# Second products ahead of the transpose in the expert stage of a graph-attention and mixture-of-experts kernel

## What is computed

```python
x = x + _L0_gnn_ref(_layernorm(x), adj, W, b_W, a_vec, b_a)          # graph attention
x = x + _L0_ffn_ref(_layernorm(x)[None], gate_w, gate_b, w1, w2, w3)[0]

# _L0_ffn_ref: 16 experts, hidden width 256, the two best experts of each token
logits = x @ gate_w + gate_b
top_probs, top_idx = top_k(softmax(logits), 2)       # normalized to a sum of 1
h1, h2 = x @ w1[e], x @ w2[e]                        # 128 -> 256, each expert
hidden = silu(h1) * h2
expert_out = hidden @ w3[e]                          # 256 -> 128
out = sum over the token's two experts of weight * expert_out
```

## Time and profile before

| | |
|---|---|
| median of the three runs | 1666.96 us (1665.37 to 1672.87) |
| the profiled execution | 1668.2 us, span 1666.4 us |
| mean granted TensorE clock | 0.985 |
| TensorE busy | 1474.4 us, 88% |
| VectorE busy | 1383.7 us, 83% |
| ScalarE busy | 822.7 us, 49% |
| GpSimd busy | 523.5 us, 31% |
| DMA | 226 GB/s over the span |

### The profile page before, as it was taken

How to read it: one execution, slowest core, us unless ns; L and a number is a source line. 1 busy time by engine, 2 the same in 40 slices (tenths; PEclk the granted TensorE clock), 3 DMA queues, 4 the chain that set the end, 5 groups by cost and what they waited for, 6 DMA issues and landing times.

```text
span 1666.4 us, 25615 instructions
## 1 busy us (share of the span) xinstructions
PE 1474.4 (88%) x8691; PEld 888.1 (53%) x8692; DVE 1383.7 (83%) x1782; ACT 822.7 (49%) x1372; POOL 523.5 (31%) x708
## 2 busy tenths in 40 slices
PE   3808999999999999999999999999999997888780
PEld 2805654554455455445544554554454467888780
DVE  5897999999999999999999998999986764333344
ACT  2704445556556555655565565556566653223230
POOL 2500000002430351326024312602353335555450
PEclk9999999999999999999999999999999999999995
DMA  9884777786787677768867774675521657777647
GB/s 341 333 323 168 258 255 249 246 256 229 240 260 253 221 257 247 249 222 271 260 220 246 253 247 153 209 248 172 193 83 39 160 157 192 228 219 234 203 154 310
DMA packets 145575, 377.32 MB, mean 226 GB/s; under 512 B 19513, under 2 KB 50937, under 8 KB 142649
## 3 DMA queue, kind: packets, MB, share of 16 engines
q1 hardware_dynamic: 125559, 342.35, 62.2%
q0 software_dynamic: 16704, 27.17, 5.7%
q10 hardware_dynamic: 3202, 6.38, 1.0%
HBM read 347.32 MB, written 32.70 MB: 228 GB/s over the span
## 4 chain that ended last, share of the span: by engine, by line
PE 56%; DVE 20%; issue 11%; POOL 5%; DMA 4%; ACT 3%; another core or an unknown queue 1%; ACTq 0%; SPq 0%; DVEq 0%; POOLq 0%
PE pair L1221 33%; DVE ring L1509 10%; PE pair L1206 9%; PE pair L1323 8%; DVE probs L1543 7%; PE pair L1332 2%; DMA X<-in_x 2%; DMA ring<-res_d 1%; POOL X L708 1%; PE pair L1233 1%; POOL ln L783 1%; POOL numT L795 1%; ACT probs L992 1%; ACT probs L1111 1%
## 5 line engine op out<-in xcount | busy, mean ns | idle before, releaser
L1221 PE MATMUL pair<-probs,X 128*128 128x512 f32 x2048 | 1005.1, 608 | 0.0
L992 ACT ACTIVATE probs<-probs,ebias 128x1024 f32<-128x1024 f32 (+1 forms) x576 | 605.5, 1052 | 530.0 <-DVE probs L1543 517.4
L1543 DVE SCALAR_TENSOR_TENSOR probs<-s1row,ns,pair 128x1024 f32<-128x1024 f32 (+1 forms) x576 | 651.6, 1157 | 50.7 <-PE pair L1206 46.3
L1509 DVE CUSTOM_DVE_ANT_0 ring<-urow,stage 128x2048 int8<-128x2048 f16 x235 | 537.2, 2288 | 4.5 <-DMA stage<-in_adj 4.4
L1206 PEld LDWEIGHTS pair<-diag,ring 128*128 128x128 fp8e5 x4096 | 266.1, 99 | 402.3 <-issue 205.7
L1221 PEld LDWEIGHTS pair<-probs,X 128*128 128x128 f32 x2048 | 344.8, 191 | 216.1 <-issue 216.1
L1206 PE MATMUL pair<-diag,ring 128*128 128x128 bf16 x4096 | 325.4, 220 | 74.4 <-ACT diag L1002 45.8
L846 POOL DMA_INDIRECT xd_d<-xres,sloti x120 | 184.5, 1537 | 39.5 <-issue 31.7
L1323 PE MATMUL pair<-probs,ring 128*128 128x128 f32 x1152 | 158.8, 282 | 39.0 <-ACT probs L1105 21.6
L1937 DVE TENSOR_TENSOR probs<-probs,pair 128x256 f32<-128x256 f32 x144 | 60.3, 419 | 145.7 <-ACT probs L1111 103.6
L921 POOL DMA_INDIRECT res_d<-ring x144 | 139.6, 969 | 127.6 <-DVE ring L1945 95.0
(11 more groups left out here) (272 smaller groups left out, 689.5 us busy)
## 6 DMA issues: line engine op xcount, KB each, us to landing
stage<-in_adj SPq DMA_DIRECT2D x470, 512.0 KB
ring<-w_d SPq DMA_DIRECT2D x144, 256.0 KB
ring<-in_adj SPq DMA_DIRECT2D x21, 1024.0 KB
ring<-xd_d SPq DMA_DIRECT2D x144, 65.0 KB
ring<-res_d SPq DMA_DIRECT2D x16, 512.0 KB, 9.9
w_d<-in_L_ffn_w SPq DMA_DIRECT2D x32, 128.0 KB, 4.4
out<-ring ACTq DMA_DIRECT2D x8, 512.0 KB, 6.8
ring<-xmid_d SPq DMA_DIRECT2D x1, 3840.0 KB
```

Source lines behind the costliest of these rows:

```text
L992: act.activation(probs[:, n % PR, 0:wide], probs[:, n % PR, 0:wide], ACT.Exp, bias=ebias[:, j:j + 1], scale=RISE).then_inc(probs_ready, 1)
L1221: m = pe.matmul(acc[q][:, lo:hi], X[:, j, :], probs[:, n % PR, lo:hi], start=(j == 0), stop=(j == NT - 1))
L1509: dve.tensor_tensor_reduce(m, urow[:, c * CH:(c + 1) * CH], edges, CODE, NO_EDGE, ALU.subtract, ALU.max, part[:, k, c:c + 1]).then_inc(pie ...
L1543: dve.scalar_tensor_tensor(out=probs[:, n % PR, 0:wide], in0=s1row[:, q, 0:wide], scalar=ns2[:, j:j + 1], in1=Tp[n % 2][:, 0:wide], op0=AL ...
```

## The change

In all three places the second products of tile i - 2 are issued before the transpose of tile i + 2. Nothing else is changed; the functions called are the same.

```diff
@@ the first 48 tiles
                 if i >= 1:
                     e[i - 1] = expert_of(i - 1)
-                t_x(i + 2, (i + 2) % XS, (i + 2) // XS + 1)
                 if i >= 2:
                     m_y(i - 2, (i - 2) % XS, e[i - 2], i - 2 < 2)
+                t_x(i + 2, (i + 2) % XS, (i + 2) // XS + 1)
@@ the loop of 16 tiles
                     e[u - 1] = expert_of(XS * g + (u - 1))
+                    m_y(i - 2, (u - 2) % XS, e[u - 2], False)
                     t_x(i + 2, (u + 2) % XS, g + 1 if u + 2 < XS else g + 2)
-                    m_y(i - 2, (u - 2) % XS, e[u - 2], False)
@@ the last 16 tiles
                 if i - 1 < ST:
                     e[i - 1] = expert_of(i - 1)
+                m_y(i - 2, (i - 2) % XS, e[i - 2], False)
                 if i + 2 < ST:
                     t_x(i + 2, (i + 2) % XS, (i + 2) // XS + 1)
-                m_y(i - 2, (i - 2) % XS, e[i - 2], False)
```

## The result

The change makes the kernel slightly slower. Its median is 1674.32 us (1670.07 to 1675.89, 16 runs) against 1668.61 us (1663.69 to 1673.21, 16 runs) of the kernel before, timed beside it. The ratio of the runs is 1.0029, with a 95% interval of 1.0016 to 1.0042. That is 4.8 us; the medians differ by 5.7. That lies inside the 0.5% that the prediction called "no change that can be told", but sixteen runs of each tell it from zero.

A forecast was written before the change was run, and what follows sets the result against it. The prediction took TensorE's work and standing still to bound the experts' tiles. Its terms, 0 + 0 + 0 + 2.5 - 0.5 = +2 us on the profiled 1668.2, gave 1670.2, or 1669 us as a median; range 1655 to 1684.

The forecast's parts named there:

- The forecast case: Whole kernel: no change that can be told, within 0.5% (8.3 us), including the change doing nothing; chance 0.60.
- The waits of the second products: TensorE, experts' tiles: second products' waits, now ahead of the transpose, cost nothing to 1 us; taken as 0.
- The later transpose while signals are prompt: Experts' tiles: transpose starts 0.44 us later, but its copy has 1.0 us of cover before its user; cost 0.
- The later transpose when signals are held: Where signals come one by one, the transpose's copy comes 0.8 us later; 0 to 8 us, taken as 2.5.
- ScalarE's idle time before L1105: ScalarE's wait before its copy of the transpose should rise from 4.7 to some 7 to 10 us.
- The earlier second products: Second products start 0.11 us earlier, so VectorE's result copies wait less; gain 0 to 1 us, taken as 0.5.
- The beat stays, nothing moves outside the stretch: Experts' tiles keep their 5.7 us beat of three tiles; attention part and last 42 us stay as they are.
- The test at 36 to 45 us of idle time before L1323: TensorE's idle time before the first products should stay there; under 30, or over 48 with L1105 as releaser, refutes the prediction.
- The slower rival: Transpose's signal comes last and ends the stall: 0.8 us per beat, measurable from 11 of 48; 1680 us, chance 0.22.
- The rival of the broken beat: Experts' tiles: new order breaks the three-tile beat more often, removing a third of TensorE's idle time; 1654 us, chance 0.18.
- What holds the signals: TensorE's signals come late when it works without a gap, 2.0 us in one beat; GpSimd's indirect DMA is a suspect.

The follow-up runs named there:

- waits_only: Kernel before with its order kept; only the second products' two waits put in front of the transpose: 1674.88 us, 0.9989 of the kernel before.
- actstore_a: Order of the change, but results stored by plain DMAs from ScalarE's queue in tile order, without scattering: 1616.29 us, 0.9644 of the kernel before.
- actstore_b: Order of before, but results stored by plain DMAs from ScalarE's queue in tile order, without scattering: 1616.77 us, 0.9645 of the kernel before.
- copy_waits_y: Kernel before, TensorE unchanged; ScalarE's copy of a transpose also waits for the second products' signal: 1680.62 us, 1.0027 of the kernel before.
- x_first: Kernel before with the transpose of tile i + 2 moved ahead of the first products of tile i: 1679.60 us, 1.0019 of the kernel before.
- pace1: Kernel before with one small GpSimd operation behind each indirect store, stores 1.49 us apart: 1660.28 us, 0.9960 of the kernel before.
- deep: Order of before, pipeline one tile longer with more buffers, ScalarE taking the SiLU ahead of the copy: 1665.65 us, 0.9943 of the kernel before.
- pace2: Kernel before with two small GpSimd operations behind each indirect store: 1696.85 us, 1.0186 of the kernel before.

## Why the prediction was right or wrong

- *The sign and the size.* Forecast +2 us, measured +4.8 us: the sign is right, and the forecast is less than half of what came. The forecast case, no change above 0.5%, is what came, and 1674.32 lies in the range of 1655 to 1684. The median of before was also 1.65 us higher in this timing (1668.61).
- *The waits of the second products, 0.* Right: 1.7 us before L1332, and `waits_only` shows no cost in its times.
- *The later transpose while signals are prompt, 0.* Right: the beat at 1506.29, and `actstore_a` against `actstore_b`.
- *The later transpose when signals are held, 2.5 us.* This is the step that was mis-sized. The mechanism is the one described, the signal of the second products overtaking that of the transpose; `copy_waits_y` reproduces the cost with it alone (and `x_first` gave no gain from the opposite). But I counted the places by what L1105 waited in the old order, eight to ten. That row says how often the copy was late when its signal came before the other, and not how often it would be when it comes behind. After the change it waited for L1316 in 41 places, 19.1 us. I also halved the term for places where something else holds the first products. Of 22 us more waiting in these profiles about a quarter, 4.8 us, reaches the end of the kernel. The upper bound, 8 us, held. But it was 10 places of 0.8 us each, and the late copies were four times as many; that most of them cost nothing was not foreseen, so the bound held by luck.
- *ScalarE's idle time before L1105 rises to 7 to 10 us.* Wrong by a factor of three, 26.6 us, for the same reason.
- *The earlier second products, -0.5 us.* No run isolates a gain. VectorE's wait before L1945 fell from 13.0 to 8.0 us as foreseen, and nobody waited for it.
- *The beat stays, nothing moves outside the stretch.* Right: 5.65 us, and the same windows.
- *The test at 36 to 45 us of idle time before L1323.* The 47.2 us missed it, and it was no good test: one profile shows one execution, and the profile of `waits_only`, whose copy is prompt and whose median is no higher, has 48.1.
- *The slower rival.* It was the same mechanism with a larger count, and it is what acts. At its price of 0.8 us, 4.8 us are six beats of 48, below the eleven from which it would have decided; most of the late copies still have cover.
- *The rival of the broken beat.* Nothing of it came by this order; rather the reverse, since the two stretches without a stall in the profile of before have no counterpart after. (The prediction counts one such stretch; another of 19.5 us begins at 1432.7.) The beat can be broken, as by `pace1`, and without the indirect stores it is not there.
- *What holds the signals.* The prediction says that they are late when TensorE works without a gap, and that they come when it has run dry. `actstore_b` has no gap and prompt signals, and `deep` lets most of them out while TensorE works: so neither holds as a rule, and it was the coincidence of one beat. Its suspect, the indirect DMA, is confirmed as far as that the lateness goes with it.
- *The page of the Trainium skill (PSUM — Partial Sum Buffer, Engine vs sequencer instructions).* It says that an increment attached to a matmul fires when this matmul completes. In `actstore_b`, where no indirect DMA runs beside it, the trace agrees to 0.03 us at 1461.74; where these run, ScalarE sees the signal 2.0 us late. The semaphore's own record is late as well, at 1507.51, so it isn't ScalarE that is slow. In a kernel of the first kind the forecast by the rule, no effect of the order, was also measured.

## What to carry to other kernels

The place of an instruction in a queue is also the place of its signal. Before work is reordered "for nothing", compare the start of each consumer with the end of its producer. Where signals come late, whatever is moved behind needs cover for that delay as well, and the wait that it has now doesn't tell what it will have. One profile can't place an effect that is smaller than the spread of a kernel's executions. And where a busy engine's consumers start late though they are idle, look at what runs beside it (here a stream of indirect DMAs on GpSimd) before turning the order round: that was worth up to 60 us (in kernels that leave the scattering out, so it is a bound and no version to take), the order 5. Of the kernels that compute everything, a deeper pipeline (0.9943) or a small gap between the stores (0.9960) beats both the kernel before and the one after.

## What the runs showed of the hardware

- Beside GpSimd's indirect DMAs, which in a row start 1.27 us apart, TensorE's signals reached ScalarE up to 2.0 us late; without them, 0.03. Of TensorE's recorded signals 75% were over 0.1 us late in the kernel before and none in `actstore_b`; ScalarE's and VectorE's came within 0.013 us in every run. The path on which they are held was not found: the stores differ from the plain ones in the engine that issues them and in how they are made, and both were changed at once.
- With the stores 1.98 us apart (`pace2`) all recorded signals of TensorE came within 0.06 us; with 1.49 us (`pace1`) 72% were still over 0.1 us late. TensorE also paused more in `pace2`.
- Held signals come out in the order in which they were made (and 1521.04 to 1522.46 above), most of them when the stores pause: 123 of the 142 that were over 0.3 us late in the kernel before came more than 1.5 us after the start of the last store. This is read from the traces, not tested.
